# A new order of work in the last stretch of a conditioned linear-attention kernel

## The reference

```python
xn = ln(x) * ln_w + ln_b
q = softmax((xn @ Wq + bq) per head, over its 64 columns)
k = softmax((xn @ Wk + bk + mask penalty), over the tokens)
v = (xn @ Wv + bv) * mask
att = einsum('bnhd,bnhl->bhdl', k, v)
y = einsum('bnhd,bhdl->bnhl', q, att)              # 2048 x 512 per batch
hh = ln(y) * ln2_w + ln2_b, times (1 + scale) plus shift, both from silu(cond) @ W_emb + b_emb
out = x + silu(hh) @ W_out + b_out
```

## Time and profile before

| what | value |
|---|---|
| median of 3 runs | 497.97 us (496.4 to 498.42) |
| the profiled execution | 496.72 us |
| its span, first to last instruction | 494.9 us |
| PE busy | 465.5 us, 94% of the span |
| DVE, ACT, POOL busy | 364.5, 265.0, 124.6 us |
| the stretch from the end of G to the last matmul | 396.9 to 491.7 us |

### The profile page before, as it was taken

The page is one execution under the profiler, slowest core; times in us unless marked ns, Lnnn a source line. Parts: engine busy times, 40 slices in busy tenths (PEclk is TensorE's granted clock), DMA queues, the critical chain, the costliest instruction groups (busy, mean ns, idle before and its releaser), DMA issues.

```text
span 494.9 us, 7296 instructions
## 1 busy us (share of the span) xinstructions
PE 465.5 (94%) x2478; PEld 370.4 (75%) x2478; DVE 364.5 (74%) x893; ACT 265.0 (54%) x487; POOL 124.6 (25%) x106
## 2 busy tenths in 40 slices
PE   4988999998899989999999999998899988999997
PEld 1666876885688768778888888887678857877765
DVE  6699976765878766879677568667998538777762
ACT  4234332321787323347556556656979635477782
POOL 0013311120100000104223333223310131456565
PEclk9999999999999999999999999999999999999999
DMA  8991110112132210110203212121321000333344
GB/s 280 360 373 51 44 42 3 43 48 101 45 126 85 86 34 10 44 42 1 86 22 128 85 44 86 44 85 67 106 88 63 1 0 23 121 103 118 127 152 147
DMA packets 23093, 43.50 MB, mean 88 GB/s; under 512 B 1992, under 2 KB 2064, under 8 KB 23056
## 3 DMA queue, kind: packets, MB, share of 16 engines
q1 hardware_dynamic: 21968, 40.93, 24.4%
q10 hardware_dynamic: 1088, 2.10, 1.1%
HBM read 34.64 MB, written 8.39 MB: 87 GB/s over the span
## 4 chain that ended last, share of the span: by engine, by line
PE 76%; DVE 15%; ACT 4%; issue 4%; DMA 1%; POOL 1%; DVEq 0%; ACTq 0%
PE ps L1067 20%; PE ps L1069 20%; PE ps L1068 20%; PE ps L1072 8%; PE ps L1228 4%; PE ps L1160 1%; ACT ps L394 1%; DVE kf L816 1%; DVE res L843 1%; DVE xst_raw L615 1%; ACT x_in L308 1%; DVE qs L716 1%; ACT kf L382 1%; PE ps L1213 1%; PE ps L1132 1%
## 5 line engine op out<-in xcount | busy, mean ns | idle before, releaser
L561 POOL TENSOR_TENSOR qs<-qs,qmax 128x512 f32<-128x512 f32 x32 | 35.9, 1121 | 199.0 <-DVE qmax L721 199.0
L1067 PE MATMUL ps<-wk_hi,zT_hi 128*128 128x512 f32 x128 | 53.7, 420 | 2.0 <-DVE kf L702 2.0
L1067 PE MATMUL ps<-ek_hi,zm_hi 128*128 128x512 f32 x128 | 50.8, 397 | 2.9 <-DVE ek_lo L757 2.1
L293 ACT ACTIVATE zT_hi<-ps 128x512 fp32r<-128x512 f32 x32 | 19.1, 597 | 64.2 <-PE ps L1072 64.1
L1067 PE MATMUL ps<-wq_hi,zT_hi 128*128 128x512 f32 x128 | 52.5, 411 | 0.3 <-DVE qs L716 0.3
L1068 PE MATMUL ps<-wk_lo,zT_hi 128*128 128x512 f32 x128 | 51.0, 398 | 0.0
L1069 PE MATMUL ps<-wk_hi,zT_lo 128*128 128x512 f32 x128 | 50.8, 397 | 0.0
L1069 PE MATMUL ps<-wq_hi,zT_lo 128*128 128x512 f32 x128 | 50.6, 395 | 0.0
L1068 PE MATMUL ps<-wq_lo,zT_hi 128*128 128x512 f32 x128 | 50.5, 395 | 0.0
L1069 PE MATMUL ps<-ek_hi,zm_lo 128*128 128x512 f32 x128 | 49.9, 390 | 0.0
L1068 PE MATMUL ps<-ek_lo,zm_hi 128*128 128x512 f32 x128 | 49.9, 390 | 0.0
(11 more groups left out here) (210 smaller groups left out, 1150.7 us busy)
## 6 DMA issues: line engine op xcount, KB each, us to landing
x_in<-in_x_dram SPq DMA_DIRECT2D x32, 512.0 KB, 3.5
res<-in_x_dram SPq DMA_DIRECT2D x32, 256.0 KB, 2.7
out_dram<-res SPq DMA_DIRECT2D x32, 256.0 KB, 2.0
y<-in_L_cond_Wk_dram ACTq DMA_DIRECT2D x2, 512.0 KB, 5.0
kf<-in_L_cond_Wq_dram ACTq DMA_DIRECT2D x1, 1024.0 KB, 7.8
eq<-in_L_cond_W_out_dram SPq DMA_DIRECT2D x1, 1024.0 KB, 9.1
wv_mod<-in_L_cond_Wv_dram SPq DMA_DIRECT2D x1, 1024.0 KB, 11.3
eq<-in_L_cond_W_emb_dram SPq DMA_DIRECT2D x4, 256.0 KB, 9.9
```

The lines of the kernel that those rows point to most:

```text
L293: act.activation(o, i, ACT.Copy, scale=scale).then_inc(s[done], 1)
L561: pool.tensor_tensor(q_heads, q_heads, qmax[:].unsqueeze(2).broadcast_to([P, H, DH]), ALU.subtract).then_inc(s["q_shift"], 1)
L1067: pe.matmul(o, a[0], bb[0], start=start, stop=False)
```

## The change

All of it lies in the last stretch.

- Held outputs: product_out(12) moves ahead of the products for the attention matrix, with out_tile(12) ahead of `att_blocks`. product_out(13) comes behind the second y, 14 behind the third, 15 behind the fourth.
- Five y (16 to 20) instead of seven are made ahead of the loop, and turns 16 and 17 instead of 16 to 18. In the loop PE makes two y behind the outputs 16 and 17 (21 and 22, then 23 and 24), and from m = 18 one, as before. It turns tile 18 behind output 16, 19 behind output 17, 20 and 21 behind output 18, and from m = 19 tile m + 3, as before.
- DVE's loop begins with silu(m + 2), then out_tile(m - 1). y_finish of the chunks that end at tiles 25, 28 and 31 is split: parts 0 and 1 behind the statistics of the chunk's last tile, parts 2 and 3 in the next pass of the loop.
- LATE = 2: tiles 30 and 31 are normalised on DVE (`normalise_late`) and not on ACT, with a semaphore yn_late of their own.

```diff
+    LATE = 2
@@ ACT
             for m in range(T + 2, 2 * T):
                 scale_shift(m)
-                if m + 1 < 2 * T:
+                if m + 1 < 2 * T - LATE:
                     normalise_y(m + 1)
                 h_high(m)
@@ DVE
+            def normalise_late(m):
+                dve.wait_ge(s["y_norm"], nth_chunk(YC, m // T, m % T))
+                dve.tensor_scalar(y_of(m), y_of(m), y_r[:, m % SR:m % SR + 1], y_shift[:, m % SR:m % SR + 1],
+                                  ALU.mult, ALU.add).then_inc(s["yn_late"], 1)
...
             state_steps(1, last_outputs)
+            out_tile(HT)
             att_blocks(1)
...
             silu(HT + 3)
             y_tile(T + 2)
             y_raw(T + 2)
-            out_tile(HT)
+            out_tile(HT + 1)
             y_tile(T + 3)
             y_raw(T + 3)
             silu(T)
             y_finish(T + 3)
+            out_tile(HT + 2)
             silu(T + 1)
-            out_tile(HT + 1)
             y_tile(T + 4)
             y_raw(T + 4)
-            out_tile(HT + 2)
-            y_tile(T + 5)
-            y_raw(T + 5)
-            y_tile(T + 6)
-            y_raw(T + 6)
             for m in range(T, 2 * T):
-                out_tile(m - 1)
                 if m + 2 < 2 * T:
                     silu(m + 2)
-
-                if m + 6 < 2 * T:
-                    y_finish(m + 6)
-                if m + 7 < 2 * T:
-                    y_tile(m + 7)
-                    y_raw(m + 7)
+                out_tile(m - 1)
+                if m >= T + 2 and m + 6 < 2 * T:
+                    y_finish(m + 6, (2, 3))
+                    if m + 6 == 2 * T - 1:
+                        for k in range(2 * T - LATE, 2 * T):
+                            normalise_late(k)
+                for k in (2 * m - T + 5, 2 * m - T + 6) if m < T + 2 else (m + 7,):
+                    if k < 2 * T:
+                        y_tile(k)
+                        y_raw(k)
+                        y_finish(k, (0, 1) if m >= T + 1 and k > T + 7 else range(4))
@@ PE
             sum_exponentials()
+            product_out(HT)
             products_att(1)
...
             product_y(T)
             product_y(T + 1)
+            product_out(HT + 1)
             product_y(T + 2)
-            product_out(HT)
-            product_y(T + 3)
+            product_out(HT + 2)
             turn_y(T)
             turn_y(T + 1)
-            product_out(HT + 1)
+            product_y(T + 3)
+            product_out(HT + 3)
             product_y(T + 4)
-            product_out(HT + 2)
-            turn_y(T + 2)
-            product_y(T + 5)
-            product_out(HT + 3)
-            product_y(T + 6)
             for m in range(T, 2 * T):
                 product_out(m)
-                if m + 3 < 2 * T:
-                    turn_y(m + 3)
-                if m + 7 < 2 * T:
-                    product_y(m + 7)
+                for k in ((m + 2,), (m + 2,), (m + 2, m + 3))[m - T] if m < T + 3 else (m + 3,):
+                    if k < 2 * T:
+                        turn_y(k)
+                for k in (2 * m - T + 5, 2 * m - T + 6) if m < T + 2 else (m + 7,):
+                    if k < 2 * T:
+                        product_y(k)
```

More of the change, by code:

```diff
@@ L189, in cond_linear_attention @@
             att_ps den_ps rz_ok att_step
-            eqT_ps eqT_ok eqT1_ps eqT1_ok y_ps y_rec y_ok ystat y_norm yn_ok ynT_ps u_ok th_ok h_ok h_hi_ok h_lo_ok
+            eqT_ps eqT_ok eqT1_ps eqT1_ok y_ps y_rec y_ok ystat y_norm yn_ok yn_late ynT_ps u_ok th_ok h_ok h_hi_ok h_lo_ok
             o_ps o_ok res_b""".split()
@@ L1232, in turn_y @@
             def turn_y(m):
-                pe.wait_ge(s["yn_ok"], m + 1)
+                if m < 2 * T - LATE:
+                    pe.wait_ge(s["yn_ok"], m + 1)
+                else:
+                    pe.wait_ge(s["yn_late"], m - 2 * T + LATE + 1)
                 if m == 0:
```

## The result

The changed kernel takes 513.62 us (median of 4 runs, 510.92 to 515.09) against 497.19 for the kernel before, a ratio of 1.033, 95% interval 1.030 to 1.036. Forecast were 506.0 and 502 to 511: the direction was right, the loss is twice the one forecast.

The account below looks back on a forecast made before the run. PE, busy 94% of the span, was taken as the bound. From y 16, 74.4 us of work and 18.0 of waits ended 8.2 us later: execution 496.72 became 504.9, the median 506.0, 1.6% slower, range 502 to 511.

Parts of the forecast that it names:

- What can be won: First y to last matmul: 87.0 us with 77.2 of PE work, so a better order can win at most 9.8 us.
- Held outputs: Start of the last stretch: spreading them keeps 4.1 us of waits against 4.6, with output 16 waiting 2.0 for out_tile(14).
- Two y behind output 16, with silu first: First two loop passes: y 22 and y 24 wait behind a silu needing the turn just made, 3.53 us each.
- Two turns behind output 18: Turn 21 waits 2.88 us for normalise(21), behind scale_shift(20) and its tanh, and about 0.2 to refill the pipe.
- Silu first and halves: Steady loop: turns 22 to 29 no longer wait; outputs 20 and 23 lose 0.37 us each, output 26 1.3.
- Two norms on DVE: Tiles 30 and 31: cost DVE 1.1 us, push silu(28) by 0.2; ACT's shorter pass is not felt further.
- The sum: From y 16 on: 407.5 + 74.4 of work + 18.0 of waits = 499.9 against 491.7, 8.2 us later.
- the clock's fall: Rival, chance 0.12: eight matmuls at the slow pace behind each new long wait lose 1.6 us, 5 us more, 511.
- The forecast's own sign of being wrong: Profile after: the three long waits shorter than 2 us each, or matmuls behind them at 0.43 us.
- paid back: Rival, chance 0.10: DVE and ACT catch up while PE stands, nothing waits behind turn 21; end at +4.2, 502.
- the three waits are not there: Rival, chance 0.08: silu(18), silu(19) and normalise(21) come early enough, so 1.9 us faster, 496.1.

Follow-up runs that it names:

- b_spread: Kernel before with held outputs spread as in the change, but seven y and turn 18 ahead of the loop, loop as before: 502.04 us, ratio 1.009.
- e1: Changed kernel with silu(m + 2) moved on DVE behind the y tiles in the first two passes of the loop: 507.28 us, ratio 1.019.
- e3: Changed kernel with silu behind the y tiles in the first two passes and normalise(21) ahead of scale_shift(20): 507.48 us, ratio 1.020.
- b_loop: Kernel before with silu ahead of out_tile and y_finish in halves on DVE, the rest as before: 498.53 us, ratio 1.002.
- b_late: Kernel before with tiles 30 and 31 normalised on DVE and not on ACT: 498.67 us, ratio 1.003.
- e8: Changed kernel with extra matmuls in all four long waits (output 16, y 22, y 24, turn 21), waits kept: 507.56 us, ratio 1.021.
- e4: Changed kernel with twelve extra matmuls ahead of the wait of y 22 and of y 24, waits kept: 509.86 us, ratio 1.025.
- e7: Changed kernel with four residual buffers and not three (RR = 4): 514.22 us, ratio 1.033.
- e5: Kernel e3 with out_tile(17) ahead of silu(20) on DVE, for that pass alone: 505.95 us, ratio 1.018.
- e2: Changed kernel with normalise(21) moved on ACT ahead of scale_shift(20): 512.28 us, ratio 1.029.
- e6: Kernel e5 with out_tile(14) ahead of y_finish(19) on DVE: 503.16 us, ratio 1.012.
- b_silu_first: Kernel before with silu(m + 2) ahead of out_tile(m - 1) on DVE in the loop: 497.72 us, ratio 1.000.
- b_halves: Kernel before with y_finish of the chunks that end at 25, 28 and 31 in two halves, one pass apart: 497.91 us, ratio 1.001.

## Why the prediction was wrong

The steps, in the order of the prediction:

- *What can be won* (9.8 us of waits from y 16 on) stands.
- *Held outputs*: forecast 4.1 us of waits against 4.6. The waits came as walked, 1.12 for y 17 (1.35 by starts) and 2.16 for output 16. What the walk didn't show is what the old outputs had covered: with turn 18 and the seven y of before behind them, the spread outputs cost 4.5 us (b_spread).
- *Two y behind output 16, with silu first*: right in place and size (3.53 walked, 3.56 measured, twice). e1 shows the cause. *Two turns behind output 18*: right in size (2.88, measured 2.90), but worth next to nothing by itself: e3 shows that silu first holds output 19 for nearly as long. I had not looked what stood behind silu(20) as I had for silu(18).
- *Silu first and halves*: the small waits of outputs 20, 23 and 26 came as 0.51, 0.50 and 1.37 (walked 0.37, 0.37, 1.3). As a benefit over the old loop it was nothing: b_loop.
- *Two norms on DVE*: 1.00 us for both in the profile after, as estimated from the earlier trace rows. The gain "is not felt further", said the walk; b_late shows a loss of 1.2 us, for which the walk had 0.2, and the two norms take from 1.00 to 2.11 us, depending on the profile.
- *The sum* is the step that failed, by a missing term. To "18.0 us" of waits it adds 74.4 us of work priced at the full clock throughout; the clock's fall stood as a rival of its own with 0.12, when it was a consequence of the same waits. What it costs is shown by e8: 6.4 us between the medians. The forecast's own sign of being wrong, matmuls at 0.43 us behind the waits, came true. (A slip of 0.2 us besides: 504.9 and 1.25 make 506.2, not 506.0.) The changed kernel's four runs say the same: at a mean clock of 0.993, 0.987, 0.986 and 0.983 they took 510.92, 512.99, 514.26 and 515.09 us, some 4 us for each hundredth. Without that share the changed kernel would be 10 us slower than before, where 8.2 were forecast; the rest is the last out_tile's wait for its residual and reaction times, read from one profile and not tested alone.
- The rival's price of 5 us, from the earlier trace rows, is near the total by luck in part. It had a string of eight behind each of the three long waits. The strings behind y 22 and y 24 came; behind turn 21's 2.90 us no profile has one (the changed kernel, e1, e4, e7), and five of seven have one behind output 16, which the rival didn't name. Forecast and rival together are 511, still under the measured 513.6. The mistake was to treat them as alternatives; *paid back* and *the three waits are not there* are refuted.

The Trainium skill ("TensorE: Matmul & The Clock Gate", section "HAM oscillation — how this bites in real kernels") says that waits between bursts of matmuls, where they are long enough, bring the clock down and are paid as slow matmuls behind them. The traces here agree in the main, with fifteen slow output matmuls in the profile after and none in e8; turn 21's wait of 2.90 us, with none behind it, shows that not every such wait is paid for.

## What to carry to other kernels

Before a step is put first in a pass, ask whether its operand was made in the same pass of another engine: everything behind it then waits with it, and on an engine in strict order that is also the work which the other engine needs next. Work held back as a cover is spent once, so lay it beside the longest chain and not beside the first gap. And price a new wait of the matrix engine twice, as its length and as the slow matmuls behind it.

## What the runs showed of the hardware

*The length of a wait alone doesn't tell whether the clock falls behind it.* Output 16 waits 2.14 to 2.16 us in the changed kernel and in e1 to e5 and e7. In the profiles of e1, e3, e4, e5 and e7 six to eight slow matmuls follow, in those of the changed kernel and of e2 none. All six y waits of 3.55 or 3.56 us (changed kernel, e2, e7) have a string of seven or eight behind them; of the four of 2.71 to 2.73 (y 24 in e1, e3, e5, e6) only e6's; of turn 21's four of 2.90 none; output 19's 2.28 in e2 has none and its 1.85 in e3 has eight. Behind waits of 1.12 us one y at 2.06 to 2.07 us and three slow output matmuls came in the profiles of b_late, b_silu_first, b_halves and b_loop, and none in the kernel before. Runs of one program differ by some us, and the clock is part of it: the 23 runs of before beside e8 lie between 496.11 at a mean clock of 0.999 and 500.21 at 0.993.

*DVE's norms take longer beside POOL.* The two tensor_scalars of `normalise_late`, DVE and then POOL, in the changed kernel, in b_late and in e7:

```profile
488.01 1.00 DVE L839 TENSOR_SCALAR kf<-kf,y_r,y_shift 128x512 f32<-128x512 f32 x2
```

```profile
476.90 1.68 DVE L838 TENSOR_SCALAR kf<-kf,y_r,y_shift 128x512 f32<-128x512 f32 x2
...
476.57 1.27 POOL L575 TENSOR_TENSOR res<-res,bo_all 128x512 f32<-128x512 f32 x1 [0.53 <-DMA res<-in_x_dram]
```

```profile
489.77 2.11 DVE L839 TENSOR_SCALAR kf<-kf,y_r,y_shift 128x512 f32<-128x512 f32 x2
...
489.85 1.29 POOL L576 TENSOR_TENSOR res<-res,bo_all 128x512 f32<-128x512 f32 x1
```

They take 1.00 us where POOL's instruction ends 0.1 to 0.2 us behind their start, as in the changed kernel, e1 to e6 and e8, and 1.68 and 2.11 where POOL's add_bias runs beside them: in both of these DVE ends 0.74 us behind POOL's end, as if the second norm, or most of it, had waited for it. The Trainium skill ("GPSIMD Engine Reference", section "8. Key points") says that POOL shares its SBUF interfaces with DVE and contends with those of DVE's instructions that are in a two-port mode or have two SBUF inputs. No run here shows in which mode the norm is; if it is such an instruction, it is cheap only while POOL is idle, and the rows agree with that. In b_late's profile it is 0.7 us, of a loss of 1.2 in the median; the link was read from the profiles, not tested by itself.
